# Graph attention and a routed FFN on one core: exponentials over two PSUM banks, projections brought out by ScalarE, router products four steps earlier

## The reference

```python
h = LN(x) @ W.T + b_W
e = (h @ a1)[:, None] + (h @ a2)[None, :] + b_a[0]
e = where(e > 0, e, 0.2 * e)
scores = where(adj > 0, e, -9e15)
x = x + softmax(scores, axis=1) @ h
xf = LN(x)
logits = xf @ Wr + br                      # 64 experts, top 2, gates by softmax of the two
for e in range(64):                        # only the chosen experts count
    out += combine[:, e:e+1] * (relu(xf @ W1[e] + b1[e]) @ W2[e] + b2[e])
x = x + out
```

## Time and profile before

| | us |
|---|---|
| median of 3 runs | 280.89 |
| range of the 3 runs | 279.63 to 281.43 |
| the profiled execution's own time | 280.6 |
| its span, first to last instruction | 278.9 |
| mean granted TensorE clock (1 = 2.4 GHz) | 0.918 |

### The profile page before, as it was taken

How to read it: one execution, slowest core, us unless ns; L and a number is a source line. 1 busy time by engine, 2 the same in 40 slices (tenths; PEclk the granted TensorE clock), 3 DMA queues, 4 the chain that set the end, 5 groups by cost and what they waited for, 6 DMA issues and landing times.

```text
span 278.9 us, 6179 instructions
## 1 busy us (share of the span) xinstructions
PE 222.4 (80%) x1849; PEld 212.8 (76%) x1849; DVE 218.6 (78%) x629; ACT 172.0 (62%) x386; POOL 166.4 (60%) x194
## 2 busy tenths in 40 slices
PE   1493399898968796886985368999999999999840
PEld 1372399798968696786984357999999999999740
DVE  4857989998999989999958733889887766766464
ACT  2743668797666585765751506878877777777400
POOL 5850011634478848888875755444888888866600
PEclk9999579999979999997998556999999999999995
DMA  6993454488474950810991113223148710100067
GB/s 162 227 199 71 79 94 79 82 211 209 139 185 89 285 179 12 292 32 19 374 418 49 59 43 91 66 57 80 42 133 321 256 41 31 40 28 24 31 199 262
DMA packets 11119, 36.88 MB, mean 132 GB/s; under 512 B 2256, under 2 KB 2832, under 8 KB 10320
## 3 DMA queue, kind: packets, MB, share of 16 engines
q0 software_dynamic: 5232, 14.98, 24.6%
q1 hardware_dynamic: 5424, 21.11, 21.6%
q10 hardware_dynamic: 432, 0.40, 0.5%
HBM read 39.36 MB, written 5.51 MB: 161 GB/s over the span
## 4 chain that ended last, share of the span: by engine, by line
PE 49%; DVE 27%; issue 9%; DMA 7%; POOL 5%; ACT 1%; SPq 1%; POOLq 0%; DVEq 0%; ACTq 0%
PE bank L1090 16%; PE bank L1102 15%; DVE arena L693 8%; PE bank L988 6%; DVE arena L699 4%; PE bank L972 4%; POOL table L419 2%; DVE arena L684 2%; DMA arena<-result 2%; DMA xs<-in_x 2%; PE bank L938 2%; DVE xs L705 2%; PE bank L1079 1%; PE bank L948 1%; DVE st L708 1%
## 5 line engine op out<-in xcount | busy, mean ns | idle before, releaser
L988 PE MATMUL bank<-arena 128*128 128x130 f32 x512 | 62.7, 279 | 1.4 <-ACT arena L542 1.3
L988 PEld LDWEIGHTS bank<-arena 128*128 128x128 f32 x512 | 60.3, 194 | 2.1 <-DVE xs L705 1.5
L1090 PE MATMUL bank<-arena 128*128 x384 | 60.4, 281 | 0.1
L1102 PE MATMUL bank<-w2s,arena 128*128 x384 | 58.8, 276 | 0.2 <-issue 0.2
L419 POOL DMA_INDIRECT table<-rows_in,pos x32 | 47.9, 1496 | 11.9 <-issue 8.1
L1090 PEld LDWEIGHTS bank<-arena 128*128 128x128 f32 x384 | 51.2, 194 | 0.5 <-issue 0.2
L1102 PEld LDWEIGHTS bank<-w2s,arena 128*128 128x128 f32 x384 | 50.6, 192 | 0.6 <-issue 0.6
L972 PE MATMUL bank<-ident,arena 128*128 128x128 f32 x256 | 35.5, 299 | 19.0 <-DVE arena L699 19.0
L868 DVE SCALAR_TENSOR_TENSOR arena<-bank,arena 128x128 f32 x96 | 33.6, 350 | 21.7 <-PE bank L1102 20.6
L972 PEld LDWEIGHTS bank<-ident,arena 128*128 128x128 f32 x256 | 32.5, 156 | 20.1 <-DVE arena L699 20.1
L601 ACT ACTIVATE arena<-bank,arena 128x128 f32<-128x128 f32 x96 | 35.1, 366 | 18.1 <-PE bank L1090 16.9
(11 more groups left out here) (190 smaller groups left out, 274.1 us busy)
## 6 DMA issues: line engine op xcount, KB each, us to landing
arena<-in_adj POOLq DMA_DIRECT2D x16, 512.0 KB, 5.4
w2s<-in_w SPq DMA_DIRECT2D x8, 768.0 KB, 4.6
arena<-in_w SPq DMA_DIRECT2D x6, 1024.0 KB, 9.2
arena<-in_w SPq DMA_DIRECT2D x4, 512.0 KB, 4.9
w2s<-in_w SPq DMA_DIRECT2D x4, 512.0 KB, 3.8
xs<-in_x SPq DMA_DIRECT2D x4, 256.0 KB, 6.3
arena<-result SPq DMA_DIRECT2D x2, 512.0 KB, 4.3
arena<-result SPq DMA_DIRECT2D x4, 256.0 KB, 6.1
```

Source lines behind the costliest of these rows:

```text
L988: ins = pe.matmul(OB[t % 2][:, 0:D + 2], pt_r[:, t % 2, j, :], h[:, j, :], start=(j == 0), stop=(j == T - 1))
L1090: ins = pe.matmul(hp(p, b), w1u[:, p % UW, P * b:P * b + P], xT_all[:, bass.ds(column, P)], start=True, stop=True)
L1102: ins = pe.matmul(yp(p), hT[:, p % UH, b, :], w2s[:, bass.ds(u, 1), b, :].rearrange("p e d -> p (e d)"), start=(b == 0), stop=(b == HB - 1))
```

## The change

It has five parts. (1) Banks 0 to 3 become two tensors of two banks each, and evac takes two exponentials of 128x1024 instead of four of 128x512; each gives `s_ea` two counts. ACT's router copy stands between the two. (2) The projections come out on ACT, not DVE. PE adds the bias by a product of one row of ones with the bias row. PE does all four rows of scores first and then all projections. ACT takes chunks 0 and 1 before its scores(0), chunks 2 to 7 before its scores(1); the column s8 is made on ACT in two pieces. (3) The last four tiles of normalized x are made on DVE behind penalty(0), not on ACT; the transpose xhT moves to a slot of `pt_r`; the adjacency loads 2 and 3 are issued by POOL behind its fourth rstd; DVE's constants for the table (L780 to L788) move ahead of its first statistics. (4) route_b comes after 4 of the 16 products, not after 8. (5) POOL's writes(2,9) move behind rstd_of(6), DVE's place(3) ahead of residual(14), and route_c(4) ahead of route_b(5).

```diff
-    PLACED = [..., (2, 8, 15), (2, 9, 15)]
+    PLACED = [..., (2, 8, 15)]
-        xh, xhT = z_r[:, 1, :]..., z_r[:, 2, :]
+        xh, xhT = z_r[:, 1, :]..., pt_r[:, 1, :, :].rearrange("p t i -> p (t i)")
+        twin = [... psum_tensor(f"twin{i}", [P, 1024], F32) for i in range(2)]
...
-                if c < 3:
-                    load(c + 1)
+                if c == 0:
+                    load(1)
+            load(2)
+            load(3)
...
             rstd_of(6)
+            place(2, 9)
             rstd_of(7)
...
-            scale(3)
...
+            def h_evac(c):
+                act.wait_ge(s_h, c + 1)
+                act.activation(h[:, 2 * c:2 * c + 2, 0:D + 1], bank[4 + c % 4]..., ACT.Copy).then_inc(s_hs, 1)
+            def slope(t0, t1):
+                act.wait_ge(s_hs, t1 // 2)
+                act.activation(s8[:, t0:t1], h[:, t0:t1, D], ACT.Copy, scale=1.0 - SLOPE).then_inc(s_s8, 1)
+            h_evac(0)
+            h_evac(1)
+            slope(0, 4)
...
             def scores(t):
+                if t == 1:
+                    for c in range(2, 8):
+                        h_evac(c)
+                    slope(4, T)
...
-                for b in range(4):
+                for b in range(2):
...
-                    act.wait_ge(s_pt, 4 * t + b + 1)
+                    act.wait_ge(s_pt, 4 * t + 2 * b + 2)
...
-                    act.activation(pt_r[... CB * b:CB * b + CB ...], bank[b][:, :], ACT.Exp, scale=-1.0).then_inc(s_ea, 1)
+                    act.activation(pt_r[... 2 * CB * b:2 * CB * b + 2 * CB ...], twin[b][:, :], ACT.Exp, scale=-1.0).then_inc(s_ea, 2)
...
             xT_evac(0)
-            xT_evac(1)
             penalty(0)
+            dve.wait_ge(s_nm, 4)
+            for t in range(12, T):
+                ins = dve.tensor_scalar(xh[:, t, :], xs[:, t, :], rstd[:, t:t + 1], nm2[:, t:t + 1], ALU.mult, ALU.add)
+            ins.then_inc(s_norm3, 1)
+            xT_evac(1)
             xT_evac(2)
-            ... h_evac(0) to h_evac(7), s8, the table's constants
...
             leaky(T - 1)
+            place(3)
             residual(T - 2)
-            place(3)
...
+                        pe.matmul(at, xhT[:, P * t:P * t + P], wt_s[:, :], start=True, stop=False)
+                        ins = pe.matmul(at, ones_f[0:1, :], hbias[0:1, :], start=False, stop=True)
...
+            scores_row(0)
+            turn_x(2)
+            scores_row(1)
+            turn_x(3)
+            scores_row(2)
+            scores_row(3)
+            pe.wait_ge(s_set, 1)
             for b in range(4):
+                project(b)
...
-                        if j == T // 2 and t == LAST[q] + 2:
+                        if j == T // 4 and t == LAST[q] + 2:
                             route_b(q)
...
             route_a(5)
+            route_c(4)
             route_b(5)
-            route_c(4)
```

More of the change, by code:

```diff
@@ L102, in build @@
         zl = xT_all[:, 0:TOPK * T * D].rearrange("p (k t d) -> p k t d", k=TOPK, t=T)
-        xh, xhT = z_r[:, 1, :].rearrange("p (t d) -> p t d", t=T), z_r[:, 2, :]
+        xh, xhT = z_r[:, 1, :].rearrange("p (t d) -> p t d", t=T), pt_r[:, 1, :, :].rearrange("p t i -> p (t i)")
         s8 = sb("s8", [P, T])
@@ L177, in build @@
         nm2 = sb("nm2", [P, T])
-        bank = [ctx.enter_context(nc.psum_tensor(f"bank{i}", [P, 512], F32)) for i in range(8)]
+        twin = [ctx.enter_context(nc.psum_tensor(f"twin{i}", [P, 1024], F32)) for i in range(2)]
+        bank = [twin[i // 2][:, 512 * (i % 2):512 * (i % 2) + 512] for i in range(4)]
+        bank += [ctx.enter_context(nc.psum_tensor(f"bank{i}", [P, 512], F32)) for i in range(4, 8)]
         OB, M0, M1 = bank[4:6], bank[6], bank[7]
@@ L534, in evac @@
             def evac(t):
-                for b in range(4):
-                    for q in range(NG):
-                        if b == 2 and t == LAST[q] + 2:
-                            route_a(q)
-                    act.wait_ge(s_pt, 4 * t + b + 1)
+                for b in range(2):
+                    if b == 1:
+                        for q in range(NG):
+                            if t == LAST[q] + 2:
+                                route_a(q)
+                    act.wait_ge(s_pt, 4 * t + 2 * b + 2)
                     if t >= 2:
                         act.wait_ge(s_o, t - 1)
-                    act.activation(pt_r[:, t % 2, CB * b:CB * b + CB, :].rearrange("p c i -> p (c i)"),
-                                   bank[b][:, :], ACT.Exp, scale=-1.0).then_inc(s_ea, 1)
+                    act.activation(pt_r[:, t % 2, 2 * CB * b:2 * CB * b + 2 * CB, :].rearrange("p c i -> p (c i)"),
+                                   twin[b][:, :], ACT.Exp, scale=-1.0).then_inc(s_ea, 2)
             def norm(t):
@@ L676, in _ @@
             dve.memset(padrow[:, :, :], 0.0).then_inc(s_set, 1)
+            dve.wait_ge(s_pool, 4)
+            dve.wait_ge(s_set, 1)
+            dve.tensor_scalar(sidx[0:P // 2, :], pidx[0:P // 2, :], 2.0, None, ALU.mult)
+            dve.tensor_scalar(sidx[P // 2:P, :], pidx[P // 2:P, :], 2.0, 1.0 - P, ALU.mult, ALU.add)
+            for into in (r_lo, r_hi, r_blk):
+                dve.tensor_copy(into[E:E + 1, :], iota_p[E:E + 1, 0:TAB])
+            for k in range(1 + TOPK):
+                ins = dve.tensor_scalar(padrow[:, k, ID_COL:ID_COL + 1], pidx[:, :], float(DUMP + (E + (k - 1) * P if k else 0)), None, ALU.add)
+            ins.then_inc(s_rows, 1)
             for c in range(4):
@@ L765, in _ @@
             xT_evac(0)
+            penalty(0)
+            dve.wait_ge(s_nm, 4)
+            for t in range(12, T):
+                ins = dve.tensor_scalar(xh[:, t, :], xs[:, t, :], rstd[:, t:t + 1], nm2[:, t:t + 1], ALU.mult, ALU.add)
+            ins.then_inc(s_norm3, 1)
             xT_evac(1)
-            penalty(0)
             xT_evac(2)
-            dve.wait_ge(s_was, 1)
-            h_evac(0)
-            h_evac(1)
             penalty(1)
-            for c in range(2, 6):
-                h_evac(c)
             scores(0)
[L776 to L788, removed]
             for s in range(1, T):
@@ L924, in turn_x @@
             def turn_x(b):
-                pe.wait_ge(s_norm, b + 1)
+                if b < 3:
+                    pe.wait_ge(s_norm, b + 1)
+                else:
+                    pe.wait_ge(s_norm3, 1)
                 for c in range(CB):
@@ L947, in project @@
                         t = 2 * c + j
-                        ins = pe.matmul(bank[4 + c % 4][:, j * (D + 1):(j + 1) * (D + 1)], xhT[:, P * t:P * t + P],
-                                        wt_s[:, :], start=True, stop=True)
+                        at = bank[4 + c % 4][:, j * (D + 1):(j + 1) * (D + 1)]
+                        pe.matmul(at, xhT[:, P * t:P * t + P], wt_s[:, :], start=True, stop=False)
+                        ins = pe.matmul(at, ones_f[0:1, :], hbias[0:1, :], start=False, stop=True)
                     ins.then_inc(s_h, 1)
```

21 lines of the change are left out of this document (6 added, 15 removed).

## The result

The changed kernel takes 288.52 us (median of 4 runs) against 281.16 before; the ratio is 1.025, 95% interval 1.019 to 1.031. A repetition of both kernels on another chip gave 1.026 (1.022 to 1.030). Forecast were 275.1 us, a ratio of 0.98, and 272.3 to 279.0 for 8 cases in 10. The profiled execution took 286.86 us with a span of 285.1.

The account below looks back on a forecast made before the run. From first scores to last leaky, attention was taken to go at DVE's pace. Start 3.8, loop 1.3 and tail 0.6 sum to 5.7 us off the profiled 280.6, giving 275.1 us; 8-in-10 range 272.3 to 279.0.

Parts of the forecast that it names:

- the price of a chunk: PE's projections of two tiles with bias products, eight passes: 1.0 us, bounds 0.6 and 2.0.
- part 2: DVE's list behind scores(0), projections moved to ACT: leaky(1) ready 4.0 to 4.4 us earlier, if ACT can follow.
- Rival (b): Projections on PE at slow pace, or ACT's turn-taking with PE, hold low(1): 283.5 or 284.5 us, chance 0.07.
- point of decision (32.1): Rival (b) decides from the point at which h_evac(7), ACT's last projection copy, ends later than 32.1 us.
- Part 1: Row term at the start: PE loses projects 0 to 2, scores(0) starts near 20.5 instead of 23.27, 2.8 us earlier.
- The start: Part 1 and part 2 together, up to the loop: 3.8 us gained, between 2.5 and 4.4.
- rival (a): PE idles between turn(0) and attend(0), its clock falls, the start gives little: 277.2 to 278.5 us, chance 0.17.
- Part 3: The loop: wide exponentials cost nothing in the DVE-bound part, earlier router products gain 1.3 us, 0 to 1.6.
- The router's four steps: Router products four steps earlier in attend shorten DVE's waits for logits at two groups: 1.3 us, 0 to 1.6.
- Part 4: The tail: rstd(6) moved ahead, taking 2.75 us under leaky(15); last table writes 0.6 us earlier, -0.5 to 1.2.
- The experts: Code behind attention and the gathers, unchanged: every gain ahead of the tail moves them as a block.

Follow-up runs that it names:

- e2: Changed kernel with the bias product at full height, 128 rows of 1/128 instead of one row of ones: 282.22 us, ratio 0.988 to the kernel before.
- e1: Changed kernel without the bias products (h lacks the bias and its score constant): 281.3 us, ratio 0.986 to the kernel before.
- e5: Changed kernel with ACT's copies of chunks 2 to 7 and s8's second part moved behind its second scores: ratio 1.020 to the kernel before.
- e4b: Changed kernel without bias products, DVE adding the bias to x; repeat of e4 on the third chip: 274.29 us, ratio 0.978 to the kernel before.
- e8: Kernel before with the edits of e6 and e7 together, so the change without its new start: 277.73 us against 277.82 for e7, ratio 0.9922.
- e7: Kernel before with router products after 4 of 16 and the three moves behind the loop, narrow exponentials: ratio 0.9923, 2.2 us faster.
- e6: Kernel before with one edit, two exponentials of 128x1024 a tile instead of four of 128x512: ratio 1.0042.
- c1: Kernel before, unchanged, profiled once more on the second chip: one run of 281.64 us, span 279.8.
- e3: Changed kernel with one bias product of 258 columns a chunk, 8 one-row products instead of 16: 288.06 us, ratio 1.011 to the kernel before.
- e4: Changed kernel without bias products, DVE adding the bias to x and ACT the score's constant, first chip: 280.69 us, ratio 0.984 to the kernel before.
- c2: Changed kernel again, unaltered, as control on the third chip: 287.04 us, ratio 1.026 to the kernel before.

## Why the prediction was wrong

**The step that failed** is the price of a chunk in part 2: "with the bias product it has eight, which I price at the same pass time, 1.0 us (lower bound 0.6 ..., upper bound 2.0, the slow pace)". Measured were 1.67 us at 2.4 GHz and 2.91 at 1.2 GHz, within the bounds at first, far beyond the upper one later. The pass time was right, even a little high: e2 shows 0.22 a product and 0.9 us a chunk. Missing was what lies between two products of different height, 0.19 us a step, 32 steps, 6 us. And the reason given for the fast pace was false: "PE works without a break from 12 us on". It did, and the clock fell all the same. The 16 tiles took 20.3 us (18.59 to 38.93); at 2.4 GHz throughout they would have taken 16 times 0.83, 13.3 us, without the steps 7.1. So the steps cost 6.2 us and the lower clock 7.0. PE's stretch of projections was the narrowest place, and I had said so: even by my prices DVE was to wait 0.3 us for low(1), so there was no margin at all.

The Trainium skill, TensorEngine Tiling (Array Packing), Key Properties, says that changing the tiling mode drains TensorE. Steps of 0.19 us between 1-row and 128-row weights, gone when both have 128 rows, agree with this; that the one-row product runs in another mode is not something that a trace here shows. The rule gives no price, so it could have told me to look for a cost between the products, not how large it is.

**Rival (b)**, given 0.07, is what happened: "h_evac(7) would end not at 28.4 but at 36, low(1) at 39". They ended at 39.4 and 42.2, and the leaky after that started 7.2 us late, not 3.9. Its point of decision (32.1) was passed. Its time was 283.5 to 284.5; measured were 288.5 on the median and 286.9 in the profiled run. Of its two causes the first came near: it asked for 2 us a chunk, and the eight chunks took 2.54 on average. But it named only the slow pace (7.0 us of PE's excess) and not the steps (6.2). The second cause, ACT's turn-taking through `s_hs`, cost nothing visible, since in e1 the same order works, and e5 shows that another order on ACT wins 0.6%, no more. And the argument against it, that PE doesn't stop, was the reason for the 0.07.

**Part 1** held: scores(0) at 19.42, forecast 20.5. Part of the microsecond more is luck: the second row already ran at the fast pace (L950 took 1.07 us at 15.38, where before the slow pace lasted beyond 17), while in e5 the same row took 1.91 and scores(0) came at 20.46. Over all profiles the old start has scores(0) at 21.8 to 23.3 and the new one at 19.4 to 20.5; the middle values are 2.4 us apart, forecast 2.8. The normalization on DVE hid as forecast, and penalty(2) didn't wait for its load; that the loads take 4 us each was put too high, since three of them landed near 16.8, 19.3 and 21.7 in the kernel before.

**Part 2, without the bias products**, held as well: leaky(1) at 29.77 in e4b and 30.04 in e1, forecast 31.1 to 31.4. The start was to bring 3.8 us; e4b takes 6.1 us off, e8, which lacks the new start, 2.2, so it brought about 4. The low clock that rival (a) feared did come, in turn(0), which took 3.68 us at 27.10 in e4b behind idle stretches of PE, and still the start kept its gain.

**Part 3**: a wide exponential was priced at 1.03 alone and 2.0 a pair; measured 1.01 (29.59 in e4b) and 1.94. The 0.43 in that price stood in none of the rows, which give 0.48 for a further 512 columns; measured are 0.41. The cost in the loop was counted as nothing. In the change, where the router's products come earlier, the medians of e7 and e8 bear that out. In e6, where they don't, it came to 1.2 us, in part by way of the logits: I had taken the 0.43 us out of the router's gain but not asked what it does without the earlier products. The router's four steps were worth 1.3 us by forecast; the logits' waits in the changed kernel are 2.0 instead of 4.4, of which 0.33 remain at each of the first two groups: 0.9 us there.

**Part 4**: rstd(6) under leaky(15) took 2.75 us, as forecast, and started as soon as its input was there:

```profile
143.54 2.35 DVE L722 SCALAR_TENSOR_TENSOR arena<-arena,tneg 128x2048 f32<-128x2048 f32 x1
143.72 2.75 POOL L407 TENSOR_TENSOR rstd<-ve,expo 128x2 f32<-128x2 f32 x1 [1.45 <-DVE ve L738]
...
156.31 1.02 POOL L424 DMA_INDIRECT table<-rows_in,pos  x1 [0.39 <-DVE pos L778]
```

From the end of the last leaky to the first of the nine last writes it is 10.4 us (145.89 to 156.31), before 11.4 (140.48 to 151.85): 0.9 us gained, forecast 0.6. Parts 3 and 4 together, forecast 1.9 us, measured 2.2 in e8.

**The experts** were to move as a block. Between the two profiled executions 4.5 us of the 6.2 are there at the first gather (169.47 against 165.00); from there to the end it is 115.6 us against 113.9, with the same code. The kernel before shows as much by itself, 113.9 in one profile and 115.1 in c1, so this part isn't the change's.

So the other terms of the sum came out within a microsecond: about 4 us for the start (forecast 3.8) and 2.2 for the rest (1.9). The version without the failed term, e4b, measures 0.978 where 0.98 was forecast.

## What to carry to other kernels

A small product isn't small on TensorE when it stands between large ones: adding a bias row by a one-row product in each of 16 tiles cost 0.19 us a step and then the clock. Give it full height (e2), use fewer and wider ones (e3), or move the bias to where another engine waits (e4). And price an operation that the trace doesn't show by what it does to its neighbours too: the upper bound must hold its worst pace on an engine whose list everybody waits for.

A single wait of 12 us can hide behind two engines. The way to the cause led from DVE's wait over ACT's list to PE; e5 shows that reordering the engine named in the wait only moves it.

## What the runs showed of the hardware

- A step between weights of 1 row and of 128 rows takes 0.19 us at 2.4 GHz in fp32, for 129 and for 258 columns (e2, e3, changed kernel); the load of the weights behind a step isn't hidden under the product before it, while between weights of 128 rows it starts 0.11 us ahead (e2). At 1.2 GHz a product took 0.73 us between such steps.
- TensorE's granted clock fell from 2.4 to 1.2 GHz, near 22.3 us in the changed kernel (22.6 in c2, 24.2 in e5) and at about 26.5 in e3, while the profile shows PE busy in all of the window; with full-height weights (e2) it stayed. The rows count the steps as busy: of 0.83 us a tile in the changed kernel, 0.45 are the products by e2's pace. Which quantity the chip looks at is open. The Trainium skill, TensorE: Matmul & The Clock Gate (Why this matters for your kernels), advises against idle gaps between bursts; here there were none by the profile, so keeping PE busy was not enough.
- On one chip all four profiled kernels (e1 to e4) had DVE waits of 2.5 and 2.9 to 3.6 us marked remote at the same two instructions, and the kernel before, not profiled there, took 286.3 us, against 280.3 on the two later chips. None of the other profiles has them. Their cause is open.
